# A two-layer transformer on one core: six weight folds of the second attention run behind the first experts, and the guard rows are copied from an input

## The reference

```python
x = x + attn_a(_layernorm(x), ...)   # linear attention, 16 heads of 8, elu+1 features, then an MLP 128-512-128
x = x + ffn(_layernorm(x), ...)      # softmax attention over 16 positions, 4 heads, then a mixture of 8 experts
x = x + attn_b(_layernorm(x), ...)   # attention without softmax, 16 heads of 64, bias and Wo
x = x + ffn(_layernorm(x), ...)      # the same weights as the second block

# in ffn, after its attention and a layer norm; y are the tokens, W1 (8,128,512), W2 (8,512,128)
idx = argmax(y @ Wg.T)               # one expert of 8 for each token
for e in range(8):
    out = out + (idx == e) * (relu(y @ W1[e] + b1[e]) @ W2[e] + b2[e])
```

## Time and profile before

| | |
|---|---|
| median of 3 runs | 805.21 us (804.89 to 805.32) |
| profiled execution: its time, its span | 807.94 us, 806.0 us |
| PE busy | 664.6 us (82%) |
| DVE busy | 553.9 us (69%) |
| POOL busy | 475.2 us (59%) |
| ACT busy | 335.1 us (42%) |
| DMA, mean rate over the span | 61 GB/s |

### The profile page before, as it was taken

The page is one execution under the profiler, slowest core; times in us unless marked ns, Lnnn a source line. Parts: engine busy times, 40 slices in busy tenths (PEclk is TensorE's granted clock), DMA queues, the critical chain, the costliest instruction groups (busy, mean ns, idle before and its releaser), DMA issues.

```text
span 806.0 us, 18935 instructions
## 1 busy us (share of the span) xinstructions
PE 664.6 (82%) x5406; PEld 566.1 (70%) x5406; DVE 553.9 (69%) x1986; ACT 335.1 (42%) x837; POOL 475.2 (59%) x1101
## 2 busy tenths in 40 slices
PE   5889999968688865799993999994778876499994
PEld 3678888844566655799992888883566665399894
DVE  2688888755699985588882344433589996477885
ACT  2323323215577731355542222221577761155551
POOL 5446646645478886077785333323258887356776
PEclk9899999998999975999996999997699996599998
DMA  7900000031231113233314000004001111222230
GB/s 212 311 24 14 15 18 13 20 83 41 45 90 39 39 44 141 60 83 88 84 47 116 15 20 20 20 20 117 1 2 40 46 47 41 85 71 77 75 78 23
DMA packets 53287, 48.92 MB, mean 61 GB/s; under 512 B 5840, under 2 KB 47740, under 8 KB 53104
## 3 DMA queue, kind: packets, MB, share of 16 engines
q1 hardware_dynamic: 45978, 34.55, 15.9%
q0 software_dynamic: 5568, 12.97, 4.5%
q10 hardware_dynamic: 1686, 0.73, 0.3%
HBM read 28.97 MB, written 19.83 MB: 61 GB/s over the span
## 4 chain that ended last, share of the span: by engine, by line
PE 34%; DVE 33%; issue 10%; POOL 8%; ACT 6%; DMA 4%; DVEq 3%; ACTq 1%; POOLq 1%; SPq 0%
PE wide L1412 4%; DVE early L1033 4%; PE wide L1385 4%; PE bank L1398 4%; DVE early L734 3%; PE bank L1254 3%; DVE hid_f L1306 3%; POOL rstd L532 2%; DVE stats L509 2%; PE wide L454 2%; DVEq L1299 2%; DVE stats L1302 2%; DVE z L536 2%; ACT z L978 2%; DVE late L1328 1%
## 5 line engine op out<-in xcount | busy, mean ns | idle before, releaser
L518 POOL TENSOR_TENSOR both_m<-stats 128x2 f32<-128x2 f32 (+1 forms) x94 | 19.1, 204 | 176.3 <-DVE stats L509 175.8
L1211 POOL TENSOR_TENSOR rstd<-var_e,half_neg 128x1 f32<-128x1 f32 x78 | 57.4, 736 | 72.5 <-DVE var_e L1316 69.0
L1254 PE MATMUL bank<-zt,late 128*128 128x128 f32 x624 | 91.4, 288 | 4.8 <-ACT late L1287 2.2
L532 POOL TENSOR_TENSOR rstd<-spread_m,half_neg 128x2 f32<-128x2 f32 (+1 forms) x94 | 86.0, 915 | 7.4
L1254 PEld LDWEIGHTS bank<-zt,late 128*128 128x128 f32 x624 | 78.4, 195 | 13.3 <-issue 6.4
L1120 POOL DMA_INDIRECT sorted_dram<-rows_e,pos x64 | 66.4, 1038 | 15.5 <-issue 15.1
L1287 ACT ACTIVATE late<-we 128x512 f32 x78 | 49.2, 631 | 30.9 <-PE bank L1254 25.0
L1033 DVE STREAM_TRANSPOSE early<-sc 32x256 f32<-32x256 f32 x128 | 55.8, 436 | 1.5
L1265 PE MATMUL wide<-late,hid_f 128*128 128x128 f32 x416 | 55.2, 276 | 0.9 <-DVE tmp L1312 0.8
L1265 PEld LDWEIGHTS wide<-late,hid_f 128*128 128x128 f32 x416 | 50.6, 192 | 1.4 <-issue 1.1
L963 ACT ACTIVATE early<-bank 32x256 f32<-32x256 f32 x128 | 47.4, 371 | 1.1
(11 more groups left out here) (259 smaller groups left out, 1936.6 us busy)
## 6 DMA issues: line engine op xcount, KB each, us to landing
rows_e<-sorted_dram SPq DMA_DIRECT2D x78, 128.5 KB
xa<-x_dram SPq DMA_DIRECT2D x9, 640.0 KB, 6.6
we<-L_ffn_W SPq DMA_DIRECT2D x16, 256.0 KB
x_dram<-xout SPq DMA_DIRECT2D x32, 128.0 KB, 1.8
sorted_dram<-hid_f SPq DMA_DIRECT2D x16, 128.5 KB, 3.2
rows_e<-L_ffn_b SPq DMA_DIRECT2D x1, 2048.0 KB
xa<-L_attn_a_x SPq DMA_DIRECT2D x3, 512.0 KB, 6.2
sorted_dram<-rows_e,pos POOLq DMA_INDIRECT x64, 2.8
```

Source lines behind the costliest of these rows:

```text
L532: nc.gpsimd.tensor_tensor(rstd[:, slot, w], spread_m[:, slot, 0, w], half_neg[:, w], ALU.pow).then_inc(rstd_made, 1)
L1211: nc.gpsimd.tensor_tensor(rstd[:, s % 3, 0:1], var_e[:, s % 3, :], half_neg[:, 0:1], ALU.pow).then_inc(g["rstd"], 1)
L1254: last = nc.tensor.matmul(to[:, (m % 2) * P:(m % 2 + 1) * P], we_t[:, c1, m * P:(m + 1) * P], zt[:, c1, 0, 0:P], start=True, stop=True)
```

## The change

- `hats_b` is no longer cut in two. All 12 folds stand behind `experts(0)`: on PE six centring folds, then the six others; on DVE the six copies (with their bias) follow the last `xout` of `experts(0)` and stand ahead of `block_b`. The raw weights are loaded where they were. PE no longer waits for the first step of the table.
- `make_guard`, its two memsets and the 16 stores by SP are gone. ACT issues two DMAs in the first attention (bodies 4 and 5), each of which copies 1.05 MB of the input `x` in DRAM to the guard rows of one `sorted_dram`. The guard rows now hold finite numbers of the input; read as a token number such a word lies beyond the tensor, so the row is dropped as before.

The core of the diff:

```diff
@@
-        hats_b1, hats_b2 = hats_b[:6], hats_b[6:]
@@
+        GUARDS_AT = (4, 5)
+
+        def write_guard(act, n):
+
+            to = sorted_dram[n][0:E * ROOM, :].rearrange("(e r) d -> e r d", r=ROOM)[:, 0:P, :]
+            finite = A["L0_attn_a_x"].rearrange("s b d -> (s b d)")[0:E * P * PAY].rearrange("(e r d) -> e r d", e=E, r=P)
+            act.dma_start(to.rearrange("e (a r) d -> e a (r d)", r=GUARD_RUN),
+                          finite.rearrange("e (a r) d -> e a (r d)", r=GUARD_RUN)).then_inc(guarded, 16)
@@ scalar, first attention, at the end of a body
+                if isinstance(i, int) and i in GUARDS_AT:
+                    write_guard(act, GUARDS_AT.index(i))
@@
-        def make_guard(pool):
-
-            nc.gpsimd.memset(pad_rows[:, :, 0:2 * D], 0.0).then_inc(pads_zeroed, 1)
-            pool.wait_ge(pads_zeroed, 1)
-            nc.gpsimd.memset(pad_rows[:, :, 2 * D:].bitcast(U32), NOWHERE).then_inc(pads_made, 1)
@@ gpsimd, attention_block
-                    if n == 0 and isinstance(i, int) and i == 5:
-                        make_guard(pool)
@@ sync, experts
-                sp.wait_ge(guarded, 16 * 2 * E)
+                sp.wait_ge(guarded, 16 * 2)
@@ sync, behind attention_block(0)
-            sp.wait_ge(pads_made, 1)
-            for n in range(2):
-                starts = sorted_dram[n][0:E * ROOM, :].rearrange("(e r) d -> e r d", r=ROOM)[:, 0:P, :]
-                for e in range(E):
-                    sp.dma_start(starts[e].rearrange("(a r) d -> a (r d)", r=PAD_RUN),
-                                 pad_rows[:, :, :].rearrange("a r d -> a (r d)")).then_inc(guarded, 16)
@@
+        table(0)
+
+        experts(0, x2_dram[:, :])
+
         @on("tensor")
         def _(pe):
             pe.wait_ge(wb_in, 16 * 3)
-            pe.wait_ge(r_step, 1)
-            hat_products(pe, hats_b1, N_F)
-        table(0)
+            hat_products(pe, hats_b, N_F)
+
+        @on("scalar")
+        def _(act):
+            hat_copies(act, hats_b, N_F)
 
         @on("vector")
         def _(dve):
-            hat_copies(dve, hats_b1, N_F, of_vector=True)
-        experts(0, x2_dram[:, :])
-
-        @on("tensor")
-        def _(pe):
-            hat_products(pe, hats_b2, N_F + len(hats_b1))
-
-        @on("scalar")
-        def _(act):
-            hat_copies(act, hats_b2, N_F + len(hats_b1))
+            hat_copies(dve, hats_b, N_F, of_vector=True)
```

More of the change, by code:

```diff
@@ L52 @@
 NOWHERE = 1 << 20
-PAD_RUN = 4
+GUARD_RUN = 4
 def pipeline(eng, n, depth, unroll, body, first):
@@ L236, in build @@
         hid_e, = parts(hid_f, (3, FC, P))
-        pad_rows, = parts(hid_f[0:P // PAD_RUN], (PAD_RUN, PAY))
         xw, fac = parts(late, (3, HB * DB), (3, HB // 2, D))
@@ L368, in build @@
         k_cleared, p_cleared = sem("k_cleared"), sem("p_cleared")
-        pads_zeroed, pads_made = sem("pads_zeroed"), sem("pads_made")
+        guarded = sem("guarded")
         @on("vector")
@@ L1123, in _ @@
                 pipeline(pool, PAIRS, DEPTH, 3, body, FIRST)
-        r_step, tabled, guarded = (sem("r_" + k) for k in ("step", "tabled", "guarded"))
+        r_step, tabled = (sem("r_" + k) for k in ("step", "tabled"))
         R_STEPS = 19
@@ L1481, in _ @@
         def _(sp):
-            sp.wait_ge(pads_made, 1)
-            for n in range(2):
-                starts = sorted_dram[n][0:E * ROOM, :].rearrange("(e r) d -> e r d", r=ROOM)[:, 0:P, :]
-                for e in range(E):
-                    sp.dma_start(starts[e].rearrange("(a r) d -> a (r d)", r=PAD_RUN),
-                                 pad_rows[:, :, :].rearrange("a r d -> a (r d)")).then_inc(guarded, 16)
-        @on("sync")
-        def _(sp):
             sp.wait_ge(m_s["att"], PAIRS)
```

## The result

| | before | after |
|---|---|---|
| median | 805.17 us (12 runs, 802.93 to 807.34) | 801.25 us (12 runs, 799.58 to 804.15) |
| profiled execution: its time, its span | 807.94 us, 806.0 us | 799.58 us, 797.8 us |
| PE busy | 664.6 us | 657.8 us |

The ratio is 0.9954, with a 95% interval of 0.9939 to 0.9969. By the medians the change is 3.9 us faster, where 2.7 were forecast. The two profiled executions lie at the edges of their runs, the one before above all 12 of them, the one after at the lowest. So the difference of their spans, 8.2 us, must not be explained as a whole. I read the difference stage by stage, and let the medians say how much of it belongs to the change.

What follows compares the result with a forecast made beforehand. Bound at the front by the table, PE's folds and DVE's copies, behind the first experts by stores and the token load. 2.3 - 1.4 + 1.8 + 0 = 2.7 us less: 805.2 to 802.5 us, range 800.3 to 804.9.

Steps and rivals of the forecast that it cites:

- The sign: Whole kernel: faster, meaning below 803.6 us, was given a chance of 0.68; the same 0.20, slower 0.12.
- Part 1: Start of the first experts: six folds on PE and six copies on DVE leave, 2.3 us back.
- the twin: The second experts, same program without folds ahead: 16.4 us from `first_row` to first `xout`, against 18.7 in the first.
- the upper bound: Start of the first experts: at most 4.8 us back, if the slow stretch were as short as 3.4 us.
- Part 2: Behind the first experts: six copies take 7.1 us after the last `xout`, so PE reaches `block_b` 1.4 us late.
- the rival of no fall: Behind the experts the clock stays full, nothing is late: 4.1 us less, 801.1 us; chance 0.2.
- The likeliest case: Behind the experts the clock falls after PE's wait of 3.3 us, and the copies keep 7.1 us; chance 0.45.
- Part 3: Start of `block_b`: PE, busy on folds until then, runs at full clock, 1.8 us back; bounds 0 to 1.8.
- The bound of nothing: Start of `block_b`: 0 us back if the clock has fallen again.
- Part 4: First attention: the guard's two DMAs fit into ACT's idle time of 3.55 us and cost nothing.
- The rule of the Trainium skill: First attention: DMAs of ACT and SP share 16 engines, so up to 12 us of transfers could delay loads ending near 42 us.
- Lost pace: Tiles of the first experts: late stores add 3.8 us, 84.3 us becoming the second experts' 88.1; 806.3 us, chance 0.12.

Runs made afterwards that it cites:

- busy_front: The changed kernel plus 20 constant products, read by nobody, on PE behind the counts at the first experts; 802.37 us, ratio 0.9959 to the kernel before.
- busy_wait: The changed kernel plus 12 constant products on PE between the second and third fold behind the experts; 801.84 us, ratio 0.9954 to the kernel before.
- folds_only: The kernel before with the folds moved as in the change but the old guard kept; 801.96 us, ratio 0.9974 to the kernel before.
- busy_front_long: The changed kernel plus 26 constant products behind the counts and 3 ahead of each of tiles 1 to 3, first experts; 799.83 us, ratio 0.9928.
- no_folds: The changed kernel without the six centring folds and their copies, raw weights loaded in their place; 800.66 us, ratio 0.9958 to the kernel before.
- no_folds_busy: As no_folds, plus 40 constant products on PE behind the other six folds, in its wait for the tokens; 798.84 us, ratio 0.9933.
- act_copies: The changed kernel with the six copies on ACT, four activations with bias each, instead of DVE; 804.33 us, ratio 0.9993 to the kernel before.
- guard_only: The kernel before with only the new guard, the folds where they were; 804.09 us, ratio 0.9996 to the kernel before.
- busy_all: The changed kernel with the filling of busy_front_long at both experts and that of busy_wait; 798.60 us, ratio 0.9922 to the kernel before.
- after_again: The changed kernel once more, unaltered, for a second profile; 801.26 us, ratio 0.9958 to the kernel before.

## Why the prediction was right

The sign was right, and 801.25 us lies in the range of 800.3 to 804.9, 1.25 us under the forecast of 802.5. By its steps:

- **Part 1, the front, forecast 2.3 us: right in what bounds it, mis-sized.** PE does wait from the counts to its first transpose, behind the load, and the clock is at 1.2 GHz over the first tiles. But the stage shrank by 3.5 us. The term that was mis-sized is the *front* that I took from the twin, the second experts with 16.4 us. In that one profile the slow stretch ended later than in any other, 12.2 us behind `first_row` and 8.8 behind the first transpose (I had read 8.5; 0.57 in the window of 706 to 707 puts the end at 706.9). In after it ended 5.8 us behind the first transpose. Other profiles give this twin 14.4 to 16.2 us, the kernel before itself 14.9, in step with where the stretch ends. I had given 4.8 as the upper bound from the same slow stretch, and the truth lay between. This 1.2 us is the error of the forecast. One more thing I had not seen: PE's wait for the load did not make the clock fall, since it had fallen 28 us ahead of `first_row`; the wait only left it low. In busy_front, where PE worked through most of this time, it was back at full at 320.9, and in the kernel before, with two folds there, at 321.1.
- **Part 2, behind the experts, forecast 1.4 us late: 1.2.** The six copies took 6.9 us, forecast 7.1. The fall of the clock was there, 0.9 us behind the end of PE's wait (forecast wait 3.3 us, measured 3.08); busy_wait shows that without it nothing is late, as the rival of no fall had it. In folds_only, also without a fall there, *behind* is still 11.82: PE was free and waited 1.01 us for `z`, since DVE's first statistics had waited 1.60 us for the load of the tokens. folds_only and busy_front_long show that the length of this wait doesn't settle whether the clock falls, nor how much of the folds the fall covers. The likeliest case was chosen rightly, but it is one of three.
- **Part 3, the warm start, forecast 1.8 us: 1.7.** no_folds and no_folds_busy isolate it: 17.32 against 15.43 with nothing changed but constant products. The bound of nothing was real too: folds_only had its fall there. What I had not thought of lies outside my bounds: a fall just behind the start costs more than a cold start (act_copies).
- **Part 4, the guard, forecast nothing: nothing**, 0.9996 (0.9984 to 1.0008), so none within about 1.3 us. The issues took 0.82 and 0.68 us inside an idle time of 3.55. The transfers show as a DMA share of 0.41 from 44 to 48 us and 0.45 from 48 to 52, where it was 0.03, and PE is busy for 4.00 and 3.98 of these 4 us:

```profile
44.00:48.00 4.00, 4.00 (x27) 3.70 (x26) 3.48 (x7) 1.71 (x5) 2.07 (x6) 1.00 0.41 136
48.00:52.00 4.00, 3.98 (x30) 3.66 (x29) 2.65 (x10) 0.85 (x3) 1.78 (x8) 1.00 0.45 191
```

  The rule of the Trainium skill, "DMA: Bandwidth & Descriptors", section "Issuing engines are not separate DMA queues", cited ahead, spoke of shared engines. The first copy does meet the last loads: from 40 to 41 us, in after, the DMA share is 1.59 at 472 GB/s. But PE's idle time ahead of its next product, at 40.41, is 1.72 us, as it was before at 42.54, so no wait for them shows.
- **Lost pace: did not happen.** The 39 tiles took 84.4 us, and 84.3 to 84.4 in all fourteen profiles. The second experts' 88.1 us belong to the second experts: every other profile shows 87.2 to 88.0 there.
- **The sum.** 3.5 - 1.2 + 1.7 = 4.0, with the median's 3.9. That the two agree so closely is in part luck: each term is read from one profile of either kernel, and guard_only shows how far one can be off. The bridge from one profiled span to the median (2.73 us taken off) was needed: without it the forecast would have been 805.2.

What stays open: what decides whether and where the clock falls behind one and the same wait of 3.08 us. I have three outcomes of it, in different kernels, and no run that steers them. Nor did I separate how much of busy_all's gain comes from the second experts.

## What to carry to other kernels

Work moved into another engine's wait is worth more or less than its duration, by what it does to the granted clock at both places: price the place that it leaves and the one that it comes to, each with the clock in short windows. A twin stage in the same trace is a good price tag, but read it in more than one profile; here the same kernel gave 16.6 in one and 14.9 in the other, more than the whole error of 1.2 us. And ahead of a chain of dependent products, an engine that finishes early and then waits can lose more than it saved: there, a few products that nobody reads are worth trying.

## What the runs showed of the hardware

- The same wait of PE, 3.08 us behind the second fold, was followed by full clock for the next four folds (3.99 us), by a fall over part of them (5.47) and over nearly all (6.58), in folds_only, after and busy_front_long.
- The fall can come late: in after PE works again from 420.17 and the clock falls at 421.1; in act_copies PE works from 434.75 and it falls at 435.7. There the wait itself is still shown at full clock, and the slow stretch lies over the work behind it. In busy_front_long it fell within the wait, at 420.1, 1.1 us ahead of PE's next product.
- There need be no long wait just ahead of a fall: in folds_only PE's longest wait between 421.80 and the fall at 433.8 is 1.01 us, and in after the clock fell at 291.4 in a stretch of 5 us (290 to 295) in which PE was busy for 3.81.
- PE busy for 20 us more made the kernel 2.7 us faster (busy_all against after_again).
- The Trainium skill, "TensorE: Matmul & The Clock Gate", in "Part 1: The HAM clock gate", says that the number of slow products varies from run to run and that the penalty of the ramp is under 1% of a typical span. The first agrees with the runs: in the two profiles of the kernel before, the same program, the slow stretch of the second front ended 12.2 and 8.9 us behind `first_row`. For the second, *start* of act_copies is 3.8 us longer than that of after, in a span of 805.4, so one slow stretch took 0.5%, as much as the change under study; what all slow stretches of the kernel cost together no run here shows.
- Two copies in DRAM of 1.05 MB each cost the issuing ACT 0.82 and 0.68 us.
- ACT's 24 activations of 128x128 with a bias ran in 7.30 us in act_copies, 0.30 each, against 0.69 to 0.74 for DVE's one copy of 128x512, so 1.22 against some 0.7 for each bank.
